# A sequence-model, attention and experts kernel: attention and experts joined into one block, with the work at their seam moved between engines

## What is computed

```python
y = _layer_norm(x + _mha(x, Wqkv, bqkv, Wo, bo), g1, be1)
z = _layer_norm(y + _moe(y, Wg, W1, b1, W2, b2), g2, be2)
# _moe: idx = argmax(xf @ Wg.T); per expert e:
#   h = relu(xf @ W1[e] + b1[e]); out += (idx == e) * (h @ W2[e] + b2[e])
...
x = x + _layernorm(_L0_attn_ref(_layernorm(x), ...))   # Mamba layer
x = x + _layernorm(_L0_ffn_ref(_layernorm(x), ...))    # attention and experts
```

## Time and profile before

| | us |
|---|---|
| time, median of 3 (lowest to highest) | 1428.22 (1427.39 to 1431.31) |
| profiled execution, its own time | 1417.69 |
| span of the profile | 1416.0 |
| PE busy | 1166.6 (82%) |
| DVE, ACT, POOL busy | 1054.1, 1015.6, 1023.5 |
| Mamba stage | 0 to about 912 |
| attention | about 914 to 1182 |
| experts | 1184 to 1416 |

### The profile page before, as it was taken

How to read it: one execution, slowest core, us unless ns; L and a number is a source line. 1 busy time by engine, 2 the same in 40 slices (tenths; PEclk the granted TensorE clock), 3 DMA queues, 4 the chain that set the end, 5 groups by cost and what they waited for, 6 DMA issues and landing times. The chain is left out here.

```text
span 1416.0 us, 29274 instructions
## 1 busy us (share of the span) xinstructions
PE 1166.6 (82%) x8861; PEld 974.4 (69%) x8861; DVE 1054.1 (74%) x2136; ACT 1015.6 (72%) x2005; POOL 1023.5 (72%) x847
## 2 busy tenths in 40 slices
PE   6698899898898898898898988457898863988850
PEld 2587787787787787787787777335665643988850
DVE  2698998899899899998989999455776661455550
ACT  3989988989889889889889888046876611556551
POOL 6598888889789888888888898422565571278776
PEclk9899999999999999999999999768999866999985
DMA  2322333323323333333322323117454333555520
GB/s 69 91 93 86 105 93 89 101 83 99 104 79 93 100 88 96 97 90 90 97 81 94 97 90 106 44 47 206 112 137 118 108 105 130 187 183 177 177 79 22
DMA packets 153862, 146.68 MB, mean 104 GB/s; under 512 B 46608, under 2 KB 105682, under 8 KB 153742
## 3 DMA queue, kind: packets, MB, share of 16 engines
q1 hardware_dynamic: 147934, 131.48, 30.9%
q0 software_dynamic: 5808, 13.81, 2.7%
HBM read 103.65 MB, written 23.24 MB: 90 GB/s over the span
## 5 line engine op out<-in xcount | busy, mean ns | idle before, releaser
L842 POOL TENSOR_TENSOR cm<-hbuf,crep 128x1024 f32<-128x1024 f32 x256 | 604.9, 2370 | 121.9 <-DVE hbuf L714 116.5
L714 DVE TENSOR_TENSOR_SCAN hbuf<-abuf,hstate,bank 128x512 f32<-128x512 f32 x512 | 614.2, 1260 | 58.2 <-PE bank L391 37.6
L596 ACT ACTIVATE abuf<-delta,aneg 128x512 f32<-128x512 f32 x512 | 337.1, 712 | 70.3 <-DVE hbuf L714 70.3
L414 PE MATMUL bank<-ident,cm 128*128 128x128 f32 x2048 | 255.8, 273 | 2.6 <-POOL cm L842 2.6
L414 PEld LDWEIGHTS bank<-ident,cm 128*128 128x128 f32 x2048 | 230.2, 142 | 3.3 <-POOL cm L842 3.3
L607 ACT ACTIVATE ub<-uT,bT 128x256 f32<-128x256 f32 x512 | 216.9, 495 | 0.3
L394 PE MATMUL bank<-ident,ub 128*128 128x128 f32 x1024 | 141.7, 279 | 24.8 <-ACT ub L607 19.4
L391 PEld LDWEIGHTS bank<-bdiag,uT 128*128 128x128 f32 x1024 | 138.2, 208 | 30.9 <-issue 17.8
L394 PEld LDWEIGHTS bank<-ident,ub 128*128 128x128 f32 x1024 | 117.2, 143 | 53.3 <-DVE hbuf L714 20.9
L391 PE MATMUL bank<-bdiag,uT 128*128 128x128 f32 x1024 | 143.3, 296 | 7.8 <-DVE hbuf L714 7.8
L311 PE MATMUL bank<-xnT,w_tap 128*128 128x512 f32 x256 | 124.8, 605 | 1.0 <-ACT halo L524 1.0
(11 more groups left out here) (225 smaller groups left out, 2043.6 us busy)
## 6 DMA issues: line engine op xcount, KB each, us to landing
crep<-c_rows SPq DMA_DIRECT2D x256, 256.0 KB, 3.2
w_of_tile<-w SPq DMA_DIRECT2D x72, 256.0 KB, 2.3
rows<-routed SPq DMA_DIRECT2D x72, 128.5 KB, 2.5
xin<-in_x SPq DMA_DIRECT2D x16, 256.0 KB, 3.7
xres<-in_x SPq DMA_DIRECT2D x16, 256.0 KB, 3.8
x_rows<-x1t SPq DMA_DIRECT2D x64, 64.0 KB, 2.1
xg<-x_rows SPq DMA_DIRECT2D x16, 256.0 KB, 3.0
v_rows<-vs SPq DMA_DIRECT2D x16, 256.0 KB
```

The costliest lines, as they stand in the source:

```text
L414: mm = pe.matmul(ps_y[j // 2][:, (j % 2 * CH + c) * P:(j % 2 * CH + c + 1) * P], cm[:, n % CM_RING, c, j * P:(j + 1) * P], ident[:, :], is ...
L596: e = act.activation(abuf[:, n % RING, c, :], delta[:, parity(g), c, :], ACT.Exp, scale=aneg[:, c, n:n + 1])
L714: dve.tensor_tensor_scan(hbuf[:, n % RING, c, :], abuf[:, n % RING, c, :], ps_bx[n % 2 * CH + c][:, :], hstate[:, bass.ds(g * (NST * CH) + ...
L842: pool.tensor_tensor(cm[:, n % CM_RING, :, :], hbuf[:, n % RING, :, :], c, ALU.mult).then_inc(s_cm, 1)
```

## The change

Attention and experts become one block: each function returns five per-engine functions, and one block calls attention's and then experts' on each engine, with no meeting of all engines between them. Their tiles are all allocated at once; `kz` and `vbd` of attention share memory (`arena`) with the rows of experts, whose ring becomes 6 quads. SP waits itself for the paddings, the scattered rows and the folded weights; PE waits for the table and the weights.

- Front: `clear` is cut in four pieces at slots -11, -6, -4 and 1; small memsets at slot 9; DVE's `fold_gate` in two steps at slots 12 and 16, PE's at slot 15; the residual matrix at slot 24, `split_biases` at slot 28.
- Drain: `fold_w1(e)` on PE at slot 62+e and on DVE at 63+e, with two banks instead of four; the residual weights at 71, 72 and 72, 73.
- Table: one tile per partition, so that the operations are 8 or 1 element wide; the sum over partitions and the turning into a row are matmuls on PE.
- Paddings: the ninth region's by one direct DMA of SP, the others by eight direct DMAs of SP at addresses from registers.
- Experts: two separate roots of 4 columns on POOL (offsets 8 and 13); `add_x1` on DVE (offset 17, ahead of `affine`); `scatter` at 17 instead of 21; `affine` and second statistics at 11 and 12 instead of 13 and 15; norms two tiles at a time at slots 9, 10 and 15, 16, behind relu.

```diff
@@ attention, sync
-            sp.wait_ge(S["experts_loaded"], 16 * len(expert_loads))
+        sp.wait_ge(S["masks_made"], 6)
+        sp.dma_start(routed[EXPERTS * CAP:, :], padrow[:, :]).then_inc(S["pad_scattered"], 16)
+        sp.wait_ge(S["table_chain"], 3)
+        for q in range(EXPERTS // 4):
+            _, end = nc.values_load_multi_w_load_instructions(padi[0:1, 4 * q:4 * q + 4], ...)
+            for e in range(4):
+                sp.dma_start(routed[bass.ds(end[e], P), :], padrow[:, :]).then_inc(S["pad_scattered"], 16)
+        sp.wait_ge(S["table_chain"], TABLE_STEPS)
@@ attention, tensor
-                if e >= 4:
-                    pe.wait_ge(S["w1_folded"], e - 3)
-                dst = banks[e % 4]
+            if e >= 2:
+                pe.wait_ge(S["w1_folded"], e - 1)
+            dst = (a0, a1)[e % 2]
...
-            fold_gate()
             for s in range(FIRST, LAST):
+            if s == 15:
+                fold_gate()
+            if 0 <= s - 62 < EXPERTS:
+                fold_w1(s - 62)
+            if s in (71, 72):
+                residual_weights(s - 71)
@@ attention, vector
                 for j in due(s, -11):
                     b_stats(j)
-                    if j == 0:
-                        clear()
+            for piece in range(4):
+                if s == (-11, -6, -4, 1)[piece]:
+                    clear(piece)
+            if s == 9:
+                clear_small()
+            if s == 12:
+                fold_gate_columns()
+            if s == 16:
                         fold_gate()
+            if s == 24:
                         residual_base()
+            if s == 28:
                         split_biases()
+            if 0 <= s - 63 < EXPERTS:
+                fold_w1(s - 63)
@@ attention, gpsimd
-            pool.wait_ge(S["pad_indices"], 1)
-            for e in range(EXPERTS + 1):
-                pool.indirect_dma_start(
-                    out=routed[:, :], out_offset=bass.IndirectOffsetOnAxis(ap=padi[:, e:e + 1], axis=0),
-                    in_=padrow[:, :], in_offset=None).then_inc(S["pad_scattered"], 16)
@@ experts, sync
+        sp.wait_ge(R["pad_scattered"], 16 * (EXPERTS + 1))
+        for i in range(4):
+            sp.wait_ge(R[f"rows_scattered{i}"], 16 * 4 * GROUPS // 4)
             load_rows(0)
+        sp.wait_ge(R["w1_folded"], EXPERTS + 2)
@@ experts, scalar
+            for t in tile(s, 1):
+                relu(t)
+            for half in range(2):
+                for q in due(s, 9 + half):
+                    norm_a(q, half)
+                for q in due(s, 15 + half):
+                    norm_b(q, half)
@@ experts, vector
+        def add_x1(q):
+            dve.wait_ge(S["z_out_ready"], q + 1)
+            if q >= 2:
+                dve.wait_ge(S[f"out_scattered{q % 2}"], 64 * (q // 2))
+            dve.tensor_copy(tokens[:, q % 2, :], rows[:, q % RINGS, :, 2 * D].bitcast(I32)).then_inc(S["res_ready"], 1)
+            dve.tensor_tensor(res[:, q % 2, :, :], z_out[:, q % 2, :, :], rows[:, q % RINGS, :, D:2 * D], ALU.add)\
+               .then_inc(S["res_ready"], 1)
...
+            for q in due(s, 17):
+                add_x1(q)
-                for q in due(s, 13):
+            for q in due(s, 11):
                     affine(q)
-                for q in due(s, 15):
+            for q in due(s, 12):
                     stats_b(q)
@@ experts, gpsimd
+            for q in due(s, 8):
+                root(0, S["variance_a"], S["roots_a"], S["zn_ready"], q)
+            for q in due(s, 13):
+                root(1, S["variance_b"], S["roots_b"], S["z_out_ready"], q)
+            for q in due(s, 17):
                     scatter(q)
```

More of the change, by code:

```diff
@@ new lines, in experts, with due, tile, quad_of @@
+    S = {n: sem("D_" + n) for n in names.split()}
+    s_rows = [sem(f"D_rows_loaded{i}") for i in range(4)]
+    FIRST, LAST = 0, TILES + 20
+    def due(s, slot):
+        q = (s - slot) // 4
+        return [q] if (s - slot) % 4 == 0 and 0 <= q < QUADS else []
+    def tile(s, slot):
+        return [s - slot] if 0 <= s - slot < TILES else []
+    def quad_of(table, q, engine, top):
+        _, four = nc.values_load_multi_w_load_instructions(
+            shared["tiles"][0:1, table, 4 * q:4 * q + 4], engines=[engine], min_val=0, max_val=top,
+            skip_runtime_bounds_check_because="the table is clamped to this range where it is made")
+        return four
@@ L1937, in build, with _ @@
                         (w["w2"][:, :, :, :], w2.rearrange("e (k p) d -> p e k d", p=P))]
-        attention(nc, sem, carrier, banks, sel, ident, half_neg, w, shared, x1, v_rows, routed, expert_loads)
-        experts(nc, sem, banks, sel, ident, half_neg, w, shared, carrier, routed, out)
-TABLE = (("order", EXPERTS), ("region", EXPERTS), ("pad", EXPERTS + 1), ("multiples", SEQS * LENGTH // P),
-         ("index", TILES))
+        arena = sb("rows_or_blocks", [P, 8 * (HEADS + BLKS) * P])
+        routes, attend = attention(nc, sem, carrier, banks, sel, ident, half_neg, w, shared, x1, v_rows, routed,
+                                   expert_loads, sb, arena)
+        expert = experts(nc, sem, banks, sel, ident, half_neg, w, shared, carrier, routed, out, sb, arena, routes)
+        block = ctx.enter_context(nc.Block())
+        @block.sync
+        def _(sp):
+            attend[0](sp)
+            expert[0](sp)
+        @block.tensor
+        def _(pe):
+            attend[1](pe)
+            expert[1](pe)
+        @block.scalar
+        def _(act):
+            attend[2](act)
+            expert[2](act)
+        @block.vector
+        def _(dve):
+            attend[3](dve)
+            expert[3](dve)
+        @block.gpsimd
+        def _(pool):
+            attend[4](pool)
+            expert[4](pool)
+TABLE_STEPS = 9
+TABLE = (("order", EXPERTS), ("region", EXPERTS), ("place", 2))
 def kernel(**inputs):
```

1645 lines of the change are left out of this document (795 added, 850 removed).

## The result

The change makes the kernel faster, by 1.4% and not by the 3.7% that were forecast. After takes 1406.44 us (median of four, 1401.73 to 1414.3), before 1427.81 beside it. The ratio is 0.9862, with a 95% interval of 0.9821 to 0.9902: -21 us where -52.5 stood in the prediction, and outside its range of 1362 to 1394. The profiled execution of after took 1406.11 us, its span is 1404.4. That is 11.6 us less than the profiled one of before, which happened to lie 10.5 us under its median; this one lies on its own, so the offset that the prediction carried over was not kept.

What follows compares the result with a forecast made beforehand. POOL was taken to bound the experts' later quads, a chain through all engines the drain. Terms -5.4 + 7 - 17.9 - 21 - 15.2 = -52.5 us gave 1365.2 profiled and, with the 10.5 offset, 1375.7 us; range 1362 to 1394.

Steps and rivals of the forecast that it cites:

- the offset that the prediction carried over: Whole kernel: the median of the runs would again stand 10.5 us above the profiled execution.
- Front, -5.4: Start of attention: earlier transposes less the cost of work moved into steady attention, -5.4 us (-6.9 to -1.9).
- The first part: Start of attention: PE's transposes no longer wait behind the gate's matmul, -6.9 us.
- the 1.5 us for the work put back: Steady attention: gate and biases on DVE cost between 0 and 5 us, taken as 1.5.
- Drain, +7: Attention's drain: eight folds of W1 ahead of the last residual lengthen it by 7 us (-1 to +13).
- Rival (b): Attention's drain: the folds bring two or three holes, +12 to +19 us, total 1388 to 1395; chance 0.15.
- Handoff, -17.9: Last routed scatter to PE's first tile: 25.4 us become 7.5, -17.9 us (-18.5 to -13).
- The landing and SP's chain: Between attention and experts: 1.5 us landing, 5.6 us from SP's start to PE, 0.4 for waits, 7.5 in all.
- the paddings: On SP: eight direct DMAs take some 6 us from about 1155, landed before POOL's last scatter.
- Steady, -21: Experts' quads: POOL relieved to 7.9 to 8.3 us, all tiles at PE's pace, -21 us (-24.4 to -12).
- Rival (a): Experts: POOL still bounds at 10.2 us per quad, nothing gained there, total 1400, or 1388 with half; chance 0.12.
- Tail, -15.2: PE's end to the span's end: 46.4 us become 31.2, POOL one behind in scatters, -15.2 us (-17 to -10).

Runs made afterwards that it cites:

- first pair: Before and after, one profiled execution each on the chip of the main result; stages from attention's first load sum to 502.1 and 488.7 us.
- second pair: The same two kernels, before and after, profiled on a second chip; their stages sum to 473.1 and 446.3 us, after's ratio 0.9817.
- combined: Changed kernel with two buffers for the experts' roots, bias split and residual base in DVE's first gaps, paddings shared by SP and ACT: ratio 0.9728.
- combined_late: Changed kernel with doubled root buffers, biases in the first gaps, paddings shared by SP and ACT, and folds behind the table: 1390.81 us, ratio 0.9823.
- direct_out_again: Repeat, with holes: changed kernel with direct instead of indirect output DMAs on POOL's queue, leaving out row placement by token: ratio 0.9668.

## Why the prediction was wrong, by its own steps

**Front, -5.4: wrong by 7 to 9 us.** The first part held: PE's transposes come 6.8 us earlier in the first pair and 6.6 in the second. The step that failed is the 1.5 us for the work put back, "nearer the free time". It compared 3.7 us of work with 15.7 us free in 50. It should have compared one block with the longest stretch for which PE can wait, and added what PE's clock loses. Its upper bound of 5 was too low as well: measured were 8.7 and 10.1 us. Of the second pair's, 7.5 to 9.0 go when the two blocks move: in `combined`, on the same chip, the 16th group starts 5.5 us earlier than in before, which is the forecast of the whole front.

**Drain, +7: right**, with +8.2 and +6.7. Without the folds there the stretch is 52.8 us instead of 60.5, so it is the folds that cost it. Rival (b), holes that add 12 to 19 us, did not come: the stretch grows by 1.5 us more with holes than without. What the prediction had no reason to ask is what the folds cost behind the table: nothing without holes, and 2 to 5 us with them.

**Handoff, -17.9: right without holes (-17.3), short with them (-12.5).** The landing and SP's chain were sized well, 8.1 us for 7.5. The failed term is the paddings: "some 6 us from about 1155" were 12.93 from 1167.12. The start was late by the front and the drain, the length by the holes, and the length decides: with 4.6 us they would have ended ahead of POOL's last scatter. The earlier trace rows had a fold held up 6.25 us with no engine named, while POOL issued its last indirect DMAs and just behind them. Rival (b) used it for DVE in the drain, and nothing asked what it does to SP.

**Steady, -21: the term that cost most, with +0.5 and -5.6.** POOL being full was right, and so was its relief. The failed step is that nothing else would hold the quads. ACT's hole stands in before too; it keeps a quad at over 10 us with POOL idle, as `combined_late` shows (10.45), and without it a quad takes 8.48, as `direct_out_again` shows. On the chips without holes after runs just as forecast, and the gain is 5.6 us because before needs 9.05 us there. Some of POOL's length in the earlier trace rows came with the holes: the shift and the copy are 0.9 us per quad longer than on the second chip. Rival (a), where POOL goes on being the bound, had the size of this term (nothing gained in the quads) for the wrong reason.

**Tail, -15.2: right in mechanism**, with -11.6 and -14.2, and most of it the add's removal. From PE's end to the span's end it is 35.1 us, not 31.2; POOL still issues its last eight indirect DMAs in one run.

**The sum.** Forecast -52.5, measured -13.4 in the stages of the first pair and -26.9 in the second. Of the 39 us missing in the first, 21.5 are the quads, 7.3 the front, 5.4 the handoff, 3.6 the tail and 1.2 the drain. The range was too narrow since no case joined a failed front with lost quads; the worst of rival (a), 1400, stood outside it by the prediction's own choice.

## What to carry to other kernels

An engine that is full is only one bound. Before counting on its relief, look for idle time on the other engines in the same period which the relief doesn't touch, above all waits that end long after what they wait for. Work put back into a pipelined loop is to be sized by its longest block against the next engine's patience, and by the clock that PE loses, not by the sum of free time. Work that fits beside a run of DMA issues is better left there, as long as nothing stalls it there.

## What the runs showed of the hardware

What an edit is worth changed from chip to chip. On three chips before took 1391 to 1392 us, and the traces have no holes. On three it took 1417 to 1428. There, while POOL issues indirect DMAs and up to 3.6 us behind the last of them, ACT, DVE or SP stand still for 0.5 to 6.3 us although what they wait for is there: ACT 2.4 to 3.5 us per quad of after, SP's eight paddings 12.7 to 14.4 instead of 4.6 us, a group of attention some 13.2 instead of 10.7. In the experts' quads the holes are gone with direct DMAs from the same queue. What makes the difference was not found. Each chip ran in one batch only, so even the chip and the moment are not told apart.
